# One more block gathered row by row, and the edge fetches of a graph layer moved ahead of it: GCN layer with routed FFN on one Trainium2 core

## The reference, cut to what matters

```python
x = x + gnn(layernorm(x), edges, W, b, prelu_a)     # 6250 nodes, 256 features, 206250 sorted edges
x = x + ffn(layernorm(x))                            # top 2 of 8 experts, one route for all tokens

def gnn(x, edge_index, ...):
    # self loops are added once more, norm = dinv[src] * dinv[dst]
    out = segment_sum((x @ W)[src] * norm[:, None], dst) + b
    return where(out > 0, out, prelu_a * out)
```

## Time and profile before

| | |
|---|---|
| time, three runs | 1107.18, 1107.53 (median), 1109.71 us |
| the profiled execution | 1105.3 us, its span 1103.8 us |
| PE, DVE, ACT, POOL busy | 97%, 77%, 61%, 54% of the span |
| second stage | 84.4 to about 782 us |
| gathers | 350 of 256 KB, 3.8 us from issue to landing (median) |
| raw edge fetches | 39 on POOL, 2.7 us from issue to landing (median) |

### The profile page before, as it was taken

How to read it: one execution, slowest core, us unless ns; L and a number is a source line. 1 busy time by engine, 2 the same in 40 slices (tenths; PEclk the granted TensorE clock), 3 DMA queues, 4 the chain that set the end, 5 groups by cost and what they waited for, 6 DMA issues and landing times.

```text
span 1103.8 us, 21022 instructions
## 1 busy us (share of the span) xinstructions
PE 1074.5 (97%) x6770; PEld 923.9 (84%) x6771; DVE 846.0 (77%) x1918; ACT 675.7 (61%) x1503; POOL 595.6 (54%) x569
## 2 busy tenths in 40 slices
PE   7999999999999999999999999999899999999997
PEld 5787888888888888888888888888699999999996
DVE  6898777778787877868777787876468787878785
ACT  5794665766666666666666666674376564646551
POOL 4102676777758776677757876580124342434332
PEclk9999999999999999999999999999999999999999
DMA  8076455566556655565646655562311111111101
GB/s 283 17 282 223 133 154 160 170 176 178 159 154 175 191 154 165 146 185 169 173 133 181 180 172 155 147 177 64 109 43 52 45 49 36 52 38 48 38 24 33
DMA packets 68438, 144.12 MB, mean 131 GB/s; under 512 B 11076, under 2 KB 36558, under 8 KB 68350
## 3 DMA queue, kind: packets, MB, share of 16 engines
q0 software_dynamic: 31808, 102.34, 32.8%
q1 hardware_dynamic: 36542, 40.66, 11.4%
HBM read 117.30 MB, written 25.67 MB: 130 GB/s over the span
## 4 chain that ended last, share of the span: by engine, by line
PE 82%; DVE 8%; ACT 4%; issue 4%; POOL 1%; DVEq 1%; DMA 0%; ACTq 0%; POOLq 0%; SPq 0%
PE banks L1777 40%; PE banks L1754 14%; PE banks L1908 11%; PE banks L1795 8%; PE banks L1895 4%; DVE gl L1339 2%; PE banks L1645 1%; PE banks L1880 1%; ACT zf L1563 1%; DVE xstats L841 1%; POOL rstdf L787 1%; ACT gf L1578 1%; PE banks L1732 1%; ACT gh L1576 1%; PE banks L1742 1%
## 5 line engine op out<-in xcount | busy, mean ns | idle before, releaser
L702 POOL DMA_INDIRECT row<-h_table,lists x350 | 405.3, 1158 | 169.2 <-issue 80.8
L1777 PE MATMUL banks<-tab,adj 128*128 128x512 f32 x1911 | 464.6, 392 | 1.1 <-ACT adj L1499 1.1
L1777 PEld LDWEIGHTS banks<-tab,adj 128*128 128x128 f32 x1911 | 357.1, 188 | 80.5 <-DVE tab L1013 1.2
L1494 ACT CAST adj<-banks 128x784 fp32r<-128x784 f32 x304 | 232.6, 817 | 239.1 <-PE banks L1754 239.1
L1114 DVE TENSOR_TENSOR hot_src<-iota_src,turned 128x1536 bf16<-128x1536 bf16 x156 | 150.6, 965 | 117.0 <-PE banks L1754 116.5
L1122 DVE TENSOR_TENSOR hot_key<-iota_key,turned 128x588 bf16<-128x588 bf16 (+1 forms) x468 | 209.6, 501 | 0.0
L1754 PEld LDWEIGHTS banks<-hot_key,hot_src 128*128 128x128 bf16 x1824 | 153.4, 145 | 40.3 <-issue 35.8
L1754 PE MATMUL banks<-hot_key,hot_src 128*128 128x147 bf16 (+1 forms) x1824 | 180.7, 248 | 0.6 <-ACT adj L1494 0.6
L1339 DVE TENSOR_TENSOR gl<-gf,gh 128x384 fp32r<-128x384 f32 (+1 forms) x136 | 117.2, 889 | 29.5 <-ACT gf L1578 29.2
L1576 ACT ACTIVATE gh<-banks,b1e 128x384 fp32r<-128x384 f32 (+1 forms) x136 | 78.3, 576 | 97.2 <-PE banks L1895 97.1
L1511 ACT ACTIVATE hot_row<-iota,own_dst 128x128 fp32r<-128x128 f32 x350 | 117.8, 406 | 0.0
(11 more groups left out here) (230 smaller groups left out, 1354.6 us busy)
## 6 DMA issues: line engine op xcount, KB each, us to landing
h_table<-tab SPq DMA_DIRECT2D x5, 2048.0 KB, 9.2
x1f<-x_dram POOLq DMA_DIRECT2D x16, 384.0 KB, 3.7
out<-res SPq DMA_DIRECT2D x48, 128.0 KB
xin<-in_x SPq DMA_DIRECT2D x45, 128.0 KB, 3.9
x_dram<-x SPq DMA_DIRECT2D x45, 128.0 KB, 2.6
row<-h_table,lists POOLq DMA_INDIRECT x350, 3.8
xs<-in_x SPq DMA_DIRECT2D x2, 1536.0 KB, 13.3
h_table<-tab SPq DMA_DIRECT2D x1, 2304.0 KB, 14.3
```

What stands on the lines that cost most here:

```text
L702: g.indirect_dma_start(out=row[:, u, :].bitcast(F32), out_offset=None, in_=h_table, in_offset=bass.IndirectOffsetOnAxis(ap=lists[:, m % 2, ...
L1494: s.copy(adj[k][:, :].rearrange("p (q n) -> p q n", n=P)[:, :, at:at + 2 * GN].rearrange("p q (b n) -> p q b n", b=2), bank_pairs[j][:, :, ...
L1777: last = mm(acc[k][:, :], adj[k][:, q * P:(q + 1) * P], tab[:, q, :], start=(at == 0), stop=(at == T - 1), skip_group_check=True)
```

## The change

Four things change together.

- `GATHERED` becomes 4, 8, 12, ... 44: eleven blocks at equal distances, so 38 dense ones remain. Each gathered block is spread over 11 steps, since three dense windows lie between two of them.
- POOL fetches the raw edges of blocks 0 and 1 into `raw` as before. Those of dense blocks 2 to 37 (36 of them) it fetches right after, in a row, into nine slots `stage` (`stage_edges`). SP stores each slot to a DRAM tensor `raw_dram` (`store_edges`), in batches between the table pieces: blocks 2 to 9 ahead of the first piece, 10 to 15 ahead of the third, 16 to 23 ahead of the fifth, 24 to 37 after the lists. POOL takes a slot again when its store has landed.
- SP loads `raw` from `raw_dram` two blocks at a time ahead of their decoding (`load_edges` on SP), so POOL no longer has fetches in the second stage. `stage` shares memory with the ring of gathered rows; hence POOL waits for every staged store before the first gather, and ACT waits for the first gathered row before its first one-hot tile.
- `add_loop` moves from POOL to DVE, between the one-hot tiles of a block's third and fourth step.

```diff
-GFIRST, GCYCLE = (5, 9), 9
+GFIRST, GCYCLE = (4,), 4
+STAGES = 9
...
+    FIRST_RAW = 2
+    STAGE_PARTS = {0: (2, 10), 2: (10, 16), 4: (16, 24)}
...
+            def store_edges(lo, hi):
+                for i in range(lo, min(hi, ND)):
+                    u, times = (i - FIRST_RAW) % STAGES, (i - FIRST_RAW) // STAGES
+                    sp.wait_ge(stage_in[u], times * 16 + 16)
+                    sp.dma_start(raw_dram[i, :, :], stage[:, u, :, :].rearrange("r p s -> r (p s)")).then_inc(staged[u], 16)
+
+            def load_edges(i):
+                u, times = (i - FIRST_RAW) % STAGES, (i - FIRST_RAW) // STAGES
+                sp.wait_ge(staged[u], times * 16 + 16)
+                sp.wait_ge(raw_free, i + 1)
+                sp.dma_start(raw[:, i % 2, :, :].rearrange("r p s -> r (p s)"), raw_dram[i, :, :]).then_inc(raw_in[i % 2], 16)
+
             with sp.If(is_dense(sp)):
-                for lo, hi in TABLE_PARTS:
+                for part, (lo, hi) in enumerate(TABLE_PARTS):
+                    if part in STAGE_PARTS:
+                        store_edges(*STAGE_PARTS[part])
+                        if part != 2:
+                            load_edges(FIRST_RAW + part // 4)
...
                 for m in range(2):
                     load_list(m)
+                store_edges(STAGE_PARTS[4][1], ND)
+                for i in range(FIRST_RAW + 2, FIRST_RAW + 5):
+                    load_edges(i)
...
+                    if d in DENSE[:ND - 5]:
+                        load_edges(DENSE.index(d) + 5)
...
+                def stage_edges(i):
+
+                    u, times = (i - FIRST_RAW) % STAGES, (i - FIRST_RAW) // STAGES
+                    if times:
+                        pool.wait_ge(staged[u], times * 16)
+                    fetch_edges(i, stage[:, u, :, :]).then_inc(stage_in[u], 16)
...
-                    if i + 1 < ND:
-                        add_loop(i + 1)
-                    if i + 4 < ND:
-                        load_edges(i + 4)
...
-                load_edges(3)
-                add_loop(0)
+                for i in range(FIRST_RAW, ND):
+                    stage_edges(i)
+                for u in range(STAGES):
+                    pool.wait_ge(staged[u], (ND - FIRST_RAW - u + STAGES - 1) // STAGES * 16)
...
                     hot_step(b, k, 2)
+                    add_loop(b - 1)
...
+                        if n == 0:
+                            act.wait_ge(row_in[0], 16)
```

More of the change, by code:

```diff
@@ L104, in gnn_ffn_kernel @@
     BY_SP = 4
+    STAGE_PARTS = {0: (2, 10), 2: (10, 16), 4: (16, 24)}
     TABLE_PARTS = ((0, 8), (HELD, 32), (8, 16), (32, 40), (16, HELD), (40, T))
     LAST = (ND - 1) % 2
-    assert DENSE[ND - 3:] == [T - 3, T - 2, T - 1] and BY_SP % 2 == 0 and DENSE[FROM + 2] + 1 >= BY_SP <= GATHERED[0] and NGATH % 2 == 0
+    assert DENSE[ND - 3:] == [T - 3, T - 2, T - 1] and BY_SP % 2 == 0 and DENSE[FROM + 2] + 1 >= BY_SP <= GATHERED[0] and NGATH % len(GFIRST) == 0
     def items(i, s):
@@ L257, in gnn_ffn_kernel @@
         xmv = room("xmv", [P, T, 2])
+        stage = room("stage", [ROWS, STAGES, P, 2], I32)
         room = tenants(RING_AT, TAB_AT)
@@ L391, in gnn_ffn_kernel @@
         x1_by_sp = [sem(f"x1_by_sp{k}") for k in range(2)]
+        raw_first = [sem(f"raw_first{i}") for i in range(FIRST_RAW)]
+        stage_in = [sem(f"stage_in{u}") for u in range(STAGES)]
+        staged = [sem(f"staged{u}") for u in range(STAGES)]
         raw_in = [sem(f"raw_in{k}") for k in range(2)]
@@ L421, in gnn_ffn_kernel @@
         dst_free = sem("dst_free")
-        rows_in = [sem(f"rows_in{u}") for u in range(U)]
+        rows_in = row_in
         loc_ready = sem("loc_ready")
@@ L675, in _, with fetch_edges, load_edges @@
                 last_row, last_edge = pool.to_reg(T * P - 1), pool.to_reg(2 * EDGES)
-                def load_edges(i):
-                    k = i % 2
-                    pool.wait_ge(raw_free, i + 1)
-                    g.indirect_dma_start(
-                        out=raw[:, k, :, :].rearrange("r p s -> r (p s)"), out_offset=None,
+                def fetch_edges(i, to):
+                    return g.indirect_dma_start(
+                        out=to.rearrange("r p s -> r (p s)"), out_offset=None,
                         in_=pairs[0:EDGES + P, :].rearrange("(r p) s -> r (p s)", p=P),
                         in_offset=bass.IndirectOffsetOnAxis(ap=starts[:, DENSE[i]:DENSE[i] + 1], axis=1),
-                        bounds_check=last_edge).then_inc(raw_in[k], 16)
-                def add_loop(i):
-                    pool.wait_ge(bank_kept, i * (STEPS * SG) + (STEPS * SG + SG))
-                    own = adj[i % 2][:, DENSE[i] * P:(DENSE[i] + 1) * P]
-                    g.tensor_tensor(own, own.bitcast(F32), ident[:, :], ALU.add).then_inc(loop_added, 1)
+                        bounds_check=last_edge)
+                def load_edges(i):
+                    pool.wait_ge(raw_free, i + 1)
+                    fetch_edges(i, raw[:, i % 2, :, :]).then_inc(raw_first[i], 16)
+                def stage_edges(i):
[3 more added lines that the diff above has]
+                    fetch_edges(i, stage[:, u, :, :]).then_inc(stage_in[u], 16)
                 def gather(n):
@@ L729, in _ @@
                 pool.wait_ge(starts_ready, 1)
-                for i in range(3):
+                for i in range(FIRST_RAW):
                     load_edges(i)
@@ L1097, in decode @@
                     source, target = raw[:, k, :, 0], raw[:, k, :, 1]
-                    dve.wait_ge(raw_in[k], b // 2 * 16 + 16)
+                    if b < FIRST_RAW:
+                        dve.wait_ge(raw_first[b], 16)
+                    else:
+                        dve.wait_ge(raw_in[k], (b - FIRST_RAW) // 2 * 16 + 16)
                     v.tensor_scalar(blk_i[:, :], source, P.bit_length() - 1, None, ALU.logical_shift_right).then_inc(decoded, 1)
@@ L1139, in own_nodes, with add_loop @@
                             v.tensor_scalar(own_dst[:, :], lists[:, m % 2, :, 1], -1.0, float(P * GATHERED[m]), ALU.mult, ALU.add).then_inc(own_dst_made, 1)
+                def add_loop(i):
+                    dve.wait_ge(bank_kept, i * (STEPS * SG) + (STEPS * SG + SG))
+                    own = adj[i % 2][:, DENSE[i] * P:(DENSE[i] + 1) * P]
+                    v.tensor_tensor(own, own.bitcast(F32), ident[:, :], ALU.add).then_inc(loop_added, 1)
                 def rows_of(b):
@@ L1183, in _ @@
                 x1_stats(T - 2, (T - 2) % 2, 0)
+                add_loop(ND - 1)
                 x1_norm(T - 2, (T - 2) % 2)
```

6 lines of the change are left out of this document (4 added, 2 removed).

## The result

| | before | changed |
|---|---|---|
| time, four runs each, median | 1108.12 us (1107.18 to 1109.71) | 1118.47 us (1117.13 to 1119.63) |
| ratio | | 1.0091, 95% interval 1.0074 to 1.0109 |
| profiled execution, span | 1103.8 us | 1115.6 us |
| first gather | 103.83 us | 117.77 us |
| last table piece lands | 98.3 us | 106.4 us |

What follows compares the result with a forecast made beforehand. The prediction took PE, busy 1074.5 of 1103.8 us, as the bound. From 1105.3 us, 7.0 saved and 7.4 of waits gave 1105.7 for the profiled execution, 1108.0 us on the median's scale, range 1101 to 1113.

Steps and rivals of the forecast that it cites:

- PE saves 7.0 us: Windows 2 to 36: one dense window fewer saves 15.9 us, eleven gathered blocks instead of ten add 8.9 us.
- The addition is hidden on DVE: Second stage: 38 additions, at most 19 us, fit into DVE's 117 us of idle time ahead of `hot_src`.
- POOL's pace suffices: Second stage: 35 gathers take POOL 51.1 us in a PE period of 55.9 us.
- Added traffic makes the sixth piece land at 101.5, and gathering starts at 112.0: End of first stage: added transfers cost 3.2 us, first gather moves from 103.83 to 112.0 us, bounds 108.9 to 114.5.
- the start is later still: Rival, first stage: SP waits for fetches, a table piece issues late, gathering starts at 116 or more, 1112 us; chance 0.09.
- The way from the sixth piece to the first gather: End of first stage: last fetches, then block 37's store, take from 101.5 to 112.0 us.
- PE waits 7.4 us, one to one with the start: Windows 2 to 4: PE waits 7.4 us for gathered rows, 4.3 if gathering starts at 108.9, 9.9 at 114.5.
- the holds: Second stage: POOL waits until its stores of blocks 0 to 3 have landed, 3.6 us each, taken as unchanged.
- an undisturbed start: Rival, first stage: gathering starts by 106, only 1.3 us of PE waits remain, 1101.8 us; chance 0.31.
- The clock falls in PE's new waits: Rival, windows 3 and 4: half clock after waits of 3 us or more costs 3.4 us, 1111.4 us; chance 0.10.
- Nothing else changes: Whole kernel: the sum held only PE's saving and PE's waits, with no term for the third stage.
- Two signs that I had named for being wrong: Profile: last table piece landing under 98 or over 104 us; granted clock under 1 in windows 3 to 5.

Runs made afterwards that it cites:

- kernels 7 and 11: 7: changed kernel with only blocks 2 to 10 staged and no POOL waits for its stores of blocks 0 to 3, 0.9966; 11: same plus 111 idle DVE instructions, 0.9942.
- kernel 1: The kernel before with only the addition moved from POOL to DVE; ratio 1.0007 to the kernel before.
- kernel 14: The changed kernel with the stores of blocks 16 to 23 moved behind the fifth table piece; ratio 1.0085 to the kernel before.
- Kernel 6: The changed kernel without POOL's waits for its stores of blocks 0 to 3; ratio 1.0018 to the kernel before.
- kernel 5: The changed kernel with only blocks 2 to 10 staged, POOL fetching the others into `raw`; ratio 0.9999 to the kernel before.
- Kernel 13: The changed kernel with 111 idle semaphore increments added to DVE's program; ratio 1.0068 to the kernel before.
- kernel 2: The kernel before with only the eleven gathered blocks, fetches and additions still on POOL; ratio 1.0046 to the kernel before.

## Why the prediction was wrong

The forecast was 1108.0 us in a range of 1101 to 1113; it took 1118.5. What failed is the start of gathering, 5.8 us later than forecast, and the assumption that nothing outside the argument changes, 2.5 us. By its own steps:

- **PE saves 7.0 us.** Right: 6.8 and 6.9 us in kernels 7 and 11, where nothing else is in the windows. The prices of the steps with rows were unchanged.
- **The addition is hidden on DVE.** Right: 38 of 0.28 us each, DVE still idles for 119 us ahead of `hot_src`, and kernel 1's windows took 664.2 us, to a tenth as before.
- **POOL's pace suffices.** Right: 385 gathers of 1.16 us, and no wait for a row after window 4.
- **Added traffic makes the sixth piece land at 101.5, and gathering starts at 112.0.** This is the step that failed: 106.4 and 117.77, above my bound of 114.5. The term for the added bytes was too small: I took 3.2 us, as if a part of them fitted into gaps, and they took 5.3 by the estimate above; a stretch with the DMA engines 96% busy had no gaps. Two terms were missing, for which I had put nothing in the sum: the first piece was issued 1.0 us later, and the engines ran partly dry for 1.8, since SP issued the fifth piece at 91.5. That chain I had as a rival, *the start is later still*, with 0.09, and worked out that the fifth piece's issue would come at 86 to 87, just in time. The second piece landed at 77.2 and not at 74, and the last of the fetches for this batch at 90.2 and not at 86 to 87. SP's own issuing was in neither sum: a small store behind the pieces takes it 1.3 us (0.3 to 0.4 ahead of them), the first one 4.4. In this kernel the fetches ended last; in kernel 14 SP's issuing alone did it. The sign stood in the earlier trace rows: the first list, small and behind two pieces, took SP 3.56 us to issue and the second 0.36, and I read only when they landed.
- **The way from the sixth piece to the first gather** was 11.4 us, where I had 10.5: nearly right. The last fetch and store took 5.35 of them (112.42 to 117.77), where I had 5.1. The 4.2 that I set beside it came from a price that the Trainium skill's page "DMA: Bandwidth & Descriptors" (Anatomy of one DMA) states for GpSimd's transfers alone, and it was too low here. So the 5.8 us of the start are 2.1 of traffic, 1.0 of the first piece's issue, 1.8 of the hole and 0.9 of this way.
- **PE waits 7.4 us, one to one with the start.** The mechanism was right: the start was 5.8 us later than forecast, which makes 13.2, and 12.9 were lost. That the two agree so closely is in part luck, since 1.5 of the 12.9 are slow clock and not waiting. Kernel 6 confirms the holds as the other half: without them 6.3 us of the 12.9 go, with the start no earlier. And kernel 5, with an early start and the holds, waited 1.9 us, where I had 1.3 for an undisturbed start. The waits fell otherwise, since rows 0 to 14 were late as well: in single pauses of 1 us from window 2 on, and not in two of 3 us.
- **The clock falls in PE's new waits.** It did, once, in window 3, for 3.4 us at 0.51 (1.2 of 2.4 GHz), during the last of four waits of 1 us in a row. I had made waits of 3 us the condition; it is not one. The slow work took 1.5 us more. Kernel 13 shows it twice in these windows, at 126.5 and 150.4 us, the second time at the end of a wait of 2.2, and kernel 14 too (126.8 and 150.7). In kernel 2 it did not fall behind a wait of 2.3, nor in kernel 6 behind two of 1.2. So the length of one wait does not tell it.
- **Nothing else changes.** Wrong, and in no rival: DVE's program grew by 17 instructions, and the jump ahead of the third stage costs 2.5 us more. Any edit on DVE in this kernel can cost or save that, the addition included. But kernel 13, the change without this cost, lies at 1115.6 us and so outside the range too; the late start by itself is enough.

So of some 10.1 us in the timed runs: -7.0 saved, +12.9 in windows 2 to 4, +2.5 at the jump, which is 8.4. The other 1.7 us are not attributed. Two signs that I had named for being wrong came: the last piece landed after 104 us, and the clock was under 1 in window 3. The first stage of the changed kernel ended 1.0 us later in its profile, and its third stage took longer than in the first profile of before by more than the jump, but both vary as much between executions of one kernel (window 2 started at 117.1 and 116.2 us, the third stage took 322.5 and 326.7 in the two profiles of before).

## What to carry to other kernels

Look first whether the stretch into which transfers move is full: with the DMA engines at 351 GB/s from the first piece to the last, every added byte cost its full time, 5.3 us of the 8.0. Then look at the order of the queue: here a small transfer behind large ones did not only land late, it held the issuing engine, and the next large one was issued into DMA engines that had run partly dry. So count the issue times of what stands between two large transfers, and the waits that it brings along; put it ahead of the first, and stage no more than free slots allow. A saving on the bounding engine is worth having only once what feeds it has its head start; here seven microseconds came back when nine blocks were staged and not 36, and when four waits that another engine already made were dropped. And where a program jumps over a branch once per launch, compare the first instruction behind the jump in both profiles ahead of any other reading: an edit that is hidden on its engine may still move the text.

## What the runs showed of the hardware

- Small stores (48 KB) on SP's queue were issued in 0.3 to 0.4 us each ahead of the table pieces, and in 1.3 us each behind two table pieces of 2 MB, the first of them in 4.4 us.
- While the table was written, the DMA engines moved 351 GB/s at 96% busy; 1.86 MB more in that stretch went with 7.1 us more, some 5.3 of them at that rate (an estimate).
- The time rose or fell by 2.3 to 2.7 us with the place of a jump's target on DVE; 17 idle instructions brought this in, and 128 in all, or 8192 bytes, took it out.
- TensorE's granted clock fell to 0.51 for 3.4 us during the last of four waits of 1 us with single matmuls between them. This row lies just ahead of the fall:

```profile
141.20:144.60 3.40, 0.93 (x2) 0.37 (x2) 2.38 (x7) 0.81 (x2) 2.79 (x3) 0.99 0.59 167
```
